# mLSTM block with a gated MLP on one core: the first heads are turned by VectorE, and the last steps of a block on TensorE stand in another order

## What is computed

```python
xn = _layernorm(x)
q, k, v, o = xn @ Wq.T, xn @ Wk.T, xn @ Wv.T, xn @ Wog.T       # 256, 256, 512, 512 features
i, f = soft_cap(xn @ Wig.T + big), soft_cap(xn @ Wfg.T + bfg)  # 8 heads
h = mlstm_scan(q, k, v, i, f)                  # a recurrence over the tokens
h_norm = (h - mean) * rsqrt(var + EPS) * gamma # per head, 64 features
y = (sigmoid(o) * h_norm) @ Wout.T
mlp = (silu(xn @ w_gate.T) * (xn @ w_up.T)) @ w_down.T
out = x + y + mlp
```

## Time and profile before

| | us |
|---|---|
| median of 3 runs | 3094.22 (3094.22 to 3095.72) |
| the profiled execution | 3095.74 |
| its span in the trace | 3094.0 |
| TensorE busy (22090 matmuls) | 3041.8 (98%) |
| VectorE busy | 2351.8 (76%) |
| ScalarE busy | 1126.9 (36%) |
| GpSimd busy | 784.4 (25%) |

### The profile page before, as it was taken

One profiled execution on the slowest core, in us unless ns is written; L12 is line 12 of the kernel. 1 busy time (PEld: TensorE's weight loads), 2 busy tenths in 40 slices (PEclk: granted clock), 3 DMA queues, 4 the chain that ended last, 5 costly groups with the idle time before them and its releaser, 6 DMA issues.

```text
span 3094.0 us, 62468 instructions
## 1 busy us (share of the span) xinstructions
PE 3041.8 (98%) x22090; PEld 2197.6 (71%) x22090; DVE 2351.8 (76%) x5913; ACT 1126.9 (36%) x2160; POOL 784.4 (25%) x1121
## 2 busy tenths in 40 slices
PE   4999999999999999999999999999999999999999
PEld 2677777777777777777777777777777777777776
DVE  7877778777777777778777787777787777787777
ACT  6333333333323333333333333333233333333332
POOL 4222222222222222222222222222222222222222
PEclk9999999999999999999999999999999999999999
DMA  5000000000000000000000000000000000000000
GB/s 225 8 14 14 14 7 7 14 14 14 14 0 14 14 14 14 7 7 14 14 14 14 7 7 14 14 14 14 0 14 14 14 14 7 7 14 14 14 14 7
DMA packets 20334, 51.09 MB, mean 17 GB/s; under 512 B 1506, under 2 KB 1634, under 8 KB 18274
## 3 DMA queue, kind: packets, MB, share of 16 engines
q1 hardware_dynamic: 20322, 50.95, 4.5%
HBM read 34.16 MB, written 16.78 MB: 16 GB/s over the span
## 4 chain that ended last, share of the span: by engine, by line
PE 97%; DVE 1%; ACT 1%; issue 0%; DMA 0%; SPq 0%; DVEq 0%; ACTq 0%
PE work L1120 21%; PE work L1121 21%; PE work L1122 21%; PE acc L1122 7%; PE acc L1121 7%; PE acc L1120 7%; PE o_bank L1232 3%; PE o_bank L1284 2%; PE work L1290 2%; PE e_bank L1265 1%; PE s_bank L1271 1%; PE work L1296 1%; PE work L1209 1%; DVE amax L760 1%; PE work L1157 1%; PE work L1256 0%
## 5 line engine op out<-in xcount | busy, mean ns | idle before, releaser
L1120 PE MATMUL work<-xt,weights 128*128 128x256 f16 x4608 | 1256.0, 273 | 0.0
L1122 PE MATMUL work<-xt,weights 128*128 128x256 f16 x4608 | 1256.0, 273 | 0.0
L1121 PE MATMUL work<-xt,weights 128*128 128x256 f16 x4608 | 1256.0, 273 | 0.0
L558 POOL TENSOR_TENSOR arena<-arena 128x256 f16<-128x256 f32 x512 | 359.4, 702 | 1610.3 <-ACT arena L692 1610.3
L1120 PEld LDWEIGHTS work<-xt,weights 128*128 128x128 f16 x4608 | 478.5, 104 | 69.2
L1121 PEld LDWEIGHTS work<-xt,weights 128*128 128x128 f16 x4608 | 450.8, 98 | 69.6
L1122 PEld LDWEIGHTS work<-xt,weights 128*128 128x128 f16 x4608 | 450.8, 98 | 52.2
L692 ACT ACTIVATE arena<-arena 128x256 f16<-128x256 f32 x512 | 213.3, 417 | 722.0 <-DVE arena L986 722.0
L688 ACT ACTIVATE arena<-work,unscale 128x256 f32<-128x256 f32 x512 | 241.2, 471 | 554.5 <-PE work L1122 554.1
L1120 PE MATMUL acc<-weights,arena 128*128 128x512 f16 x1024 | 388.1, 379 | 0.5 <-POOL arena L558 0.5
L1121 PE MATMUL acc<-weights,arena 128*128 128x512 f16 x1024 | 388.1, 379 | 0.0
(11 more groups left out here) (212 smaller groups left out, 4083.3 us busy)
## 6 DMA issues: line engine op xcount, KB each, us to landing
arena<-x_dram SPq DMA_DIRECT2D x33, 512.0 KB, 3.3
out_dram<-arena SPq DMA_DIRECT2D x32, 512.0 KB, 2.8
weights<-w_g_dram SPq DMA_DIRECT2D x4, 1024.0 KB, 12.6
weights<-w_u_dram SPq DMA_DIRECT2D x4, 1024.0 KB, 20.1
arena<-w_d_dram SPq DMA_DIRECT2D x4, 1024.0 KB, 26.6
arena<-w_qk_dram SPq DMA_DIRECT2D x1, 1024.0 KB, 5.7
arena<-w_v_dram SPq DMA_DIRECT2D x1, 1024.0 KB, 7.7
weights<-w_o_dram SPq DMA_DIRECT2D x1, 1024.0 KB, 25.1
```

Source lines behind the costliest of these rows:

```text
L558: g.tensor_tensor(hh[:, j % HB, 1, :], tt[:, j % 2, :], hh[:, j % HB, 0, :], ALU.subtract).then_inc(h_ready, 1)
L1120: t.matmul(dst, w[0], a[0], start=first, stop=False, skip_group_check=True)
L1121: t.matmul(dst, w[0], a[1], start=False, stop=False, skip_group_check=True)
L1122: return t.matmul(dst, w[1], a[0], start=False, stop=last, skip_group_check=True)
```

## The change

1. `hoT0` leaves TensorE. VectorE turns the first chunk's heads in four quarters of 4 block transposes each, `hturn00` after tile 11, `hturn01` and `hturn02` after tile 13, `hturn03` after tile 14, into a place in SBUF (`hot`). The rounding by ScalarE and the subtraction by VectorE (`hoT0`) now read this place and stand after tile 14, behind `hturn03` and ahead of tile 15's steps.
2. The two chunks' gated heads have buffers of their own (`hof`, `hof2`), and so have their fp16 parts (`ho` has a chunk axis).
3. `project(0)` moves from after tile 13 to the end of the block; `hoT1` on TensorE moves behind `down(14)`. The end of a block on TensorE is now: the products of tiles 13, 14 and 15, each with its `down(j - 2)`, then `down(14)`, the turn `hoT1`, `down(15)`, `project(0)`, `project(1)`.
4. `USES` has one use less; `att0` and `att1` take the banks 0 and 1, which are those of the next block's gates and q. `add_mlstm(i, 0)` on VectorE moves from after tile 13 to the end of the block.

```diff
--- before.py
+++ after.py
@@ -53,10 +53,11 @@
 
 
 USES = (["gates", "q", "k", "v0", "v1", "ffn0", "ffn1", "ffn2", "ffn3", "wT", "ffn4", "wbc", "ffn5", "o0",
-         "ffn6", "st0", "ffn7", "ffn8", "st1", "ffn9", "ffn10", "st2", "ffn11", "hoT0", "ffn12", "st3", "o1",
-         "ffn13", "att0", "ffn14", "ffn15", "hoT1", "att1"])
+         "ffn6", "st0", "ffn7", "ffn8", "st1", "ffn9", "ffn10", "st2", "ffn11", "ffn12", "st3", "o1",
+         "ffn13", "ffn14", "ffn15", "hoT1", "att0", "att1"])
 NUSE = len(USES)
 BANK = {name: n % 3 for n, name in enumerate(USES)}
+BANK["att0"], BANK["att1"] = 0, 1
 
 
 def bank_no(name):
@@ -89,10 +90,10 @@
 AFTER[8] = ["es2", "pv1", "center0"]
 AFTER[9] = ["scale0", "turn11"]
 AFTER[10] = ["heads0", "es3", "pv2"]
-AFTER[11] = ["hoT0", "turn12", "turn13"]
+AFTER[11] = ["turn12", "turn13", "hturn00"]
 AFTER[12] = ["pv3", "o1", "center1"]
-AFTER[13] = ["att0", "scale1"]
-AFTER[14] = ["heads1"]
+AFTER[13] = ["scale1", "hturn01", "hturn02"]
+AFTER[14] = ["heads1", "hturn03", "hoT0"]
 AFTER[15] = ["hoT1", "xT0", "xT1"]
 TURNS = 16
 
@@ -235,7 +236,7 @@
         sizes = [("qs", 512), ("qi", 512), ("kf", 512), ("kt", 512),
                  ("v", NCH * NH * VW), ("to", 512), ("pm", 1024), ("lf", 256), ("ip", 256), ("bc", 256),
                  ("mm", 256), ("upd", GW), ("num", NH * VW),
-                 ("hof", 512), ("hoh", 512), ("kp", 512), ("tt", 512), ("hh", 768), ("res", 1024),
+                 ("hof", 512), ("hof2", 512), ("hoh", 1024), ("kp", 512), ("tt", 512), ("hh", 768), ("res", 1024),
                  ("wtok", NCH * 72), ("qq", 1024), ("kk", 1024),
                  ("state", NG * GW), ("wr", 256), ("tg", 256), ("uhl", 256), ("xin", 1024)]
         at, off = {}, 0
@@ -287,11 +288,12 @@
         state = at["state"].rearrange("p (g n) -> p g n", g=NG)
         upd = at["upd"]
         num = at["num"].rearrange("p (h e) -> p h e", h=NH)
-        sq = at["hof"].rearrange("p (h e) -> p h e", h=NH)
+        sq = at["hof2"].rearrange("p (h e) -> p h e", h=NH)
         hof = at["hof"]
         qp = at["hof"].bitcast(F16).rearrange("p (a g t) -> p a g t", a=2, g=NG)
         kp = at["kp"].bitcast(F16).rearrange("p (a g t) -> p a g t", a=2, g=NG)
-        ho = at["hoh"].bitcast(F16).rearrange("p (a k t) -> p a k t", a=2, k=KC)
+        hot = arena[:, starts["bc"]:starts["bc"] + D]
+        ho = at["hoh"].bitcast(F16).rearrange("p (c a k t) -> p c a k t", c=NCH, a=2, k=KC)
         tt = at["tt"].rearrange("p (b t) -> p b t", b=2)
         HB = 3
         hh = at["hh"].bitcast(F16).rearrange("p (b a t) -> p b a t", b=HB, a=2)
@@ -532,7 +536,7 @@
 
 
             for n, started in enumerate((*work_free, out_stored, res_done, exp_done, p_ready, num_ready, ho_ready,
-                                         state_ready, xn_turned)):
+                                         state_ready, xn_turned, heads_turned)):
                 g.memset(begun[0:1, n:n + 1], 0.0).then_inc(started, START)
 
             wait_split(pool, "out", 0)
@@ -718,9 +722,12 @@
                             act.wait_ge(centered, i * NCH + k + 1)
                             s.activation(sq, num[:, :, 0:DV], ACT.Square).then_inc(squared, 1)
                         elif step.startswith("hoT"):
-                            wait_full(act, i, step)
-                            s.activation(ho[:, 0, :, :], bank(step)[:, :].rearrange("p (k t) -> p k t", k=KC),
-                                         ACT.Copy).then_inc(ho_hi, 1)
+                            if k == 0:
+                                act.wait_ge(heads_turned, START + (i + 1) * TURNS)
+                            else:
+                                wait_full(act, i, step)
+                            s.activation(ho[:, k, 0, :, :], (hot if k == 0 else bank(step)[:, :]).rearrange(
+                                "p (k t) -> p k t", k=KC), ACT.Copy).then_inc(ho_hi, 1)
                         elif step.startswith("xn"):
                             if k == 0:
                                 act.wait_ge(factors_ready, i + 2)
@@ -819,13 +826,13 @@
                 for c in range(NCH):
                     d.bn_aggr(mean_var[:, c, :], bn6[:, c, :]).then_inc(stats_ready, 1)
 
-            def turn(dst, src, q):
+            def turn(dst, src, q, done):
 
                 tokens = slice(q * 32, (q + 1) * 32)
                 for r in range(P // 32):
                     features = src[tokens, :].rearrange("t (k r f) -> t r k f", k=KC, f=32)[:, r, :, :]
                     d.transpose(dst.rearrange("p (k t) -> p k t", k=KC)[r * 32:(r + 1) * 32, :, tokens],
-                                features).then_inc(xn_turned, 1)
+                                features).then_inc(done, 1)
 
             def x_low(i, c, src):
 
@@ -1078,20 +1085,27 @@
                                                      fac.unsqueeze(2).broadcast_to((P, NH, DV)), ALU.mult))
                             own.settle(dve, i)
                             wait_drained(dve, i, f"o{k_}")
-                            d.scalar_tensor_tensor(out=hof.rearrange("p (h e) -> p h e", h=NH),
+                            d.scalar_tensor_tensor(out=(hof, at["hof2"])[k_].rearrange("p (h e) -> p h e", h=NH),
                                                    in0=to.rearrange("p (h e) -> p h e", h=NH), scalar=1.0,
                                                    in1=num[:, :, 0:DV], op0=ALU.add,
                                                    op1=ALU.mult).then_inc(ho_ready, 1)
                         elif step.startswith("hoT"):
                             dve.wait_ge(ho_hi, i * NCH + k_ + 1)
-                            d.tensor_tensor(ho[:, 1, :, :], bank(step)[:, :].rearrange("p (k t) -> p k t", k=KC),
-                                            ho[:, 0, :, :], ALU.subtract).then_inc(free_of(step), 1)
+                            ins = d.tensor_tensor(ho[:, k_, 1, :, :],
+                                                  (hot if k_ == 0 else bank(step)[:, :]).rearrange(
+                                                      "p (k t) -> p k t", k=KC),
+                                                  ho[:, k_, 0, :, :], ALU.subtract)
+                            ins.then_inc(ho_split if k_ == 0 else free_of(step), 1)
                         elif step.startswith("xT"):
                             x_low(i + 1, k_, xnt[k_])
                         elif step.startswith("turn"):
                             c = int(step[-2])
                             dve.wait_ge(xn_ready, NCH * (i + 1) + c + 1)
-                            turn(xnt[c], xn[c], k_)
+                            turn(xnt[c], xn[c], k_, xn_turned)
+                        elif step.startswith("hturn"):
+
+                            dve.wait_ge(ho_ready, START + i * NCH + 1)
+                            turn(hot, hof, k_, heads_turned)
                         elif step.startswith("kturn"):
 
                             tokens = slice(k_ * 32, (k_ + 1) * 32)
@@ -1099,12 +1113,9 @@
                                 own.step(d.transpose(
                                     k_turned.rearrange("p c g h e -> p g c h e")[tokens, :, :, h, :],
                                     kf.rearrange("p g (c t) -> p g c t", c=NCH)[h * DQ:(h + 1) * DQ, :, :, tokens]))
-                        elif step == "att0":
-                            add_mlstm(i, 0)
                 for c in range(NCH):
 
-                    if c == 1:
-                        add_mlstm(i, 1)
+                    add_mlstm(i, c)
                     dve.wait_ge(acc_full, i * NCH + c + 1)
                     wait_drained(dve, i, f"att{c}")
                     d.scalar_tensor_tensor(out=res[:, c, :], in0=acc[c][:, :], scalar=unscale[:, NS + 1:NS + 2],
@@ -1194,9 +1205,12 @@
 
                 def project(c):
 
-                    wait_drained(pe, i, f"hoT{c}")
+                    if c == 0:
+                        pe.wait_ge(ho_split, i + 1)
+                    else:
+                        wait_drained(pe, i, "hoT1")
                     for n in range(KC):
-                        mm_ = three(bank(f"att{c}")[:, :], (ho[:, 0, n, :], ho[:, 1, n, :]),
+                        mm_ = three(bank(f"att{c}")[:, :], (ho[:, c, 0, n, :], ho[:, c, 1, n, :]),
                                     (w_out[:, 0, n, :], w_out[:, 1, n, :]), n == 0, n == KC - 1)
                     mm_.then_inc(work_full, 1)
 
@@ -1241,7 +1255,7 @@
                         down(j - 2)
                     for step in AFTER[j]:
                         k = int(step[-1]) if step[-1].isdigit() else 0
-                        if step in USES:
+                        if step in USES and step != "hoT1":
                             wait_bank(pe, i, step)
                         if step == "wT":
                             pe.wait_ge(we_ready, i + 1)
@@ -1290,16 +1304,16 @@
                             t.matmul(bank(f"st{k}")[:, 0:GW], kt[:, c, g * P:(g + 1) * P],
```

(18 more changed lines are left out.)

## The result

| | us |
|---|---|
| before, median of 4 runs | 3094.97 |
| changed, median of 4 runs | 3253.57 (3252.91 to 3253.91) |
| ratio | 1.0511, 95% interval 1.0498 to 1.0524 |
| forecast | 3214, range 3165 to 3262 |

The change costs 158.6 us, 5.1%. The sign and the mechanism were as forecast, and the time lies in the range, but 39 us above the forecast: that is nearest to the rival in which the clock falls in every block (3241).

What follows compares the result with a forecast made beforehand. TensorE, busy for all 94.06 us of a block, was taken as the bound; 89.3 us of wait (transposes' saving included), 3.7 for q's bank and 27 for the clock on 3094.22 gave 3214 us, range 3165 to 3262.

Steps and rivals of the forecast that it cites:

- the rival in which the clock falls in every block: Rival, chance 0.17: TensorE's granted clock falls after the wait in every block; 3187 + 54 = 3241 us.
- Part 1: On TensorE, four transposes of 0.43 us leave each block; 13.8 us gained if nothing waits.
- Part 2: TensorE's list at the block's end: down(15) due at 1577.07; moved projection had stood where VectorE and ScalarE needed its 2.58 us.
- Part 3: VectorE's queue up to tile 15: tile 14 ready at 1574.9, before down(14) is due at 1575.34; 0.5 us to spare.
- Part 4: Tile 15's tanh queues behind the rounding of hoT0; TensorE waits 3.2 us at down(15), 2.8 us more in each block.
- Part 5: att1 lies in the bank of the next block's q, so q waits 0.12 us; 3.7 us in all.
- Part 6: TensorE's clock falls after half of the 32 waits, 1.7 us lost each time; 27 us.
- a shorter wait: Rival, chance 0.07: TensorE's wait is about half as long because VectorE is ahead of the layout somewhere; 3135 us.
- no wait: Rival, chance 0.05: tile 15 still comes in time because VectorE's transposes take a third of their length; 3084 us, faster.

Runs made afterwards that it cites:

- The kernel with the turns in VectorE's gaps: Against the kernel before: VectorE turns the first heads where it had waited, project(0) stays after tile 13, hoT1 ahead of down(14), att1 in bank 2; 3080.81 us.
- 3174.56: Changed kernel with the rounding and subtraction of the first heads (hoT0) moved behind tile 15's own steps, hturn03 still ahead of them; 3174.56 us.
- 3121.75: Changed kernel with both the last quarter turn hturn03 and hoT0 moved behind tile 15's own steps; 3121.75 us.
- the kernel with scale1 apart: Changed kernel with quarter turn hturn01 moved ahead of scale1 after tile 13, so scale1's small steps avoid GpSimd's subtraction of tile 13; 3234.28 us.

## Why the prediction was right, and where its sizes were off

- *What bounds the kernel, and where to look:* right. TensorE's full list, and tile 15 arriving just in time, decided the larger part: the wait at `down(15)`. The clock took the rest.
- *Part 1,* 0.43 us a block for the four transposes: right. The kernel with the turns in VectorE's gaps got 14.8 us where 13.8 were counted.
- *Part 2* had the steps up to `down(15)` right. Its last sentence said that the moved projection had stood where VectorE and ScalarE needed its 2.58 us. Of the kernel before that is wrong: the new order alone costs nothing (3095.7 us), so without the turns in the queue the engines need no such cover. Whether they need it with the turns in the queue is not shown.
- *Part 3,* VectorE's queue: right in order, and `down(14)` starts without a loss. But the 0.5 us that tile 14 was to have to spare were used up: 0.44 went before VectorE's second step, and TensorE's weight load waits there for GpSimd until the matmul is due. Mis-sized were the 0.44 us: `scale1` was taken from a row in which its small steps ran alone (1.27 us); in the new place one of them took 0.59 instead of 0.17. The first chunk's step in the trace of before would have shown it: its line L1067 has a minimum of 166 ns and a maximum of 597.
- *Part 4,* the wait: 3.20 forecast, 3.52 measured. The 0.44 from part 3 came on top, and 0.12 went off, since from VectorE's second step to `down(15)` it took 1654.76 - 1653.51 = 1.25 us and not 1.37. The cause was as written: two engines stand in front of tile 15, and each was shown by a run of its own (3174.56, 3121.75).
- *Part 5,* the bank: 0.12 forecast, 0.13 in the changed kernel's rows, 0.17 from the two runs that differ in it alone.
- *Part 6* is the term that was mis-sized most: 27 us forecast, 54.3 measured. The size of one fall, 1.7 us, was right. Its number was not: 32 and not 16. Half was taken because 2 of 4 waits of the setup were followed by a fall. Those were waits of 1.6 to 3.4 us in a stretch with other work around them. The wait here was above that, and with it the clock fell every time; with 3.24 us (1642.04 to 1645.72 less 0.44, in the kernel with scale1 apart) it fell in 27 of 32 blocks, with 2.25 in 10, with 0.79 in none. The Trainium skill, "TensorE: Matmul & The Clock Gate", section "HAM oscillation — how this bites in real kernels", tells of a kernel that waited in each step of its loop and was throttled back at every one. This trace agrees, with 32 falls in 32 blocks; the two runs with 3.24 and 2.25 us, whose waits recur as regularly, do not. The rival built on it gave 3241, and most of the other 12 us is the wait's 0.32 x 32 = 10.
- *The rivals* of a shorter wait and of no wait fell with the wait's 3.5 us. The one of no wait named the transposes' length as what decides; the run with the turns in gaps has no new wait at the same 0.30 us a transpose, so the length does not decide; the places of the turns, and `project(0)` back after tile 13, do.

The table's sum, 4.94 us x 32 = 158, is the whole loss; nothing is left open in size. Left open is what decides whether a wait of 2.25 or 3.24 us lowers the clock in a given block, and how the wait splits between the places of the turns and the projection's.

## What to carry to other kernels

When a step is moved off the bounding engine, its new place in the queue of the receiving engine can matter more than its length, as with one quarter turn and one rounding here (132 us): look for what stands behind it, and put it where that engine's rows show a wait. A chain that arrives just in time (a wait of 0.2 us in every round is the sign) has no room for anything ahead of it, and a rounding in ScalarE's queue that waits for VectorE holds up the tile behind it as well. Price a new wait of some 3 us on TensorE with the clock's fall on top, in every round in which it recurs: here it came in 27 to 32 of 32.

## What the runs showed of the hardware

- A wait of 3.52 us on TensorE that comes back every 99 us was followed by a fall of the granted clock from 2.4 to 1.2 GHz in 32 of 32 blocks, one of 3.24 us in 27, one of 2.25 us in 10, one of 0.79 us in none. Each fall cost 1.70 us, and 14 matmuls whose result nobody reads, put into the wait, prevented it without costing time themselves.
- A VectorE step over 8 columns with two operands from SBUF (`small<-small`) took 0.59 us when it started inside GpSimd's fp32 subtraction, until about the subtraction's end, and 0.17 us otherwise: 32 and 32 times in the kernel before, 32 and 32 with `scale1` apart, and 64 and 0 in the changed kernel. Block transposes that started inside a subtraction kept their 0.30 us (64 of them in the kernel before, 302 to 304 ns).
